# Layer norm on an x that is loaded already turned: TensorE turns the repeated means and deviations instead of x

## The reference

```python
def _layernorm(x, axis=-1, eps=1e-05):
    m = jnp.mean(x, axis=axis, keepdims=True)
    v = jnp.var(x, axis=axis, keepdims=True)
    return (x - m) / jnp.sqrt(v + eps)

# cross attention: 32 query heads, 8 key/value heads, 128 wide, rope on q and k
x = x + jnp.tanh(g_xattn[0]) * xattn(_layernorm(x), ctx, ctx, mask, wq, wk, wv, wo)
# feed-forward: 8 experts of rank 16, the best one alone is used for a token
x = x + jnp.tanh(g_ffn[0]) * ffn(_layernorm(x), route_w, A, Bw)
```

## Time and profile before

| | |
|---|---|
| median of 3 runs | 1053.44 us (1051.94 to 1054.69) |
| the profiled execution's own time | 1052.97 us |
| its span in the profile | 1051.2 us |
| TensorE busy | 1041.9 us, 99% |
| VectorE busy | 872.2 us, 83% |
| ScalarE busy | 634.0 us, 60% |
| GpSimd busy | 592.1 us, 56% |
| TensorE's granted clock | full speed throughout |

### The profile page before, as it was taken

One profiled execution on the slowest core, in us unless ns is written; L12 is line 12 of the kernel. 1 busy time (PEld: TensorE's weight loads), 2 busy tenths in 40 slices (PEclk: granted clock), 3 DMA queues, 4 the chain that ended last, 5 costly groups with the idle time before them and its releaser, 6 DMA issues.

```text
span 1051.2 us, 19131 instructions
## 1 busy us (share of the span) xinstructions
PE 1041.9 (99%) x6663; PEld 865.3 (82%) x6663; DVE 872.2 (83%) x1423; ACT 634.0 (60%) x1112; POOL 592.1 (56%) x518
## 2 busy tenths in 40 slices
PE   9999999999999999999999999999999999999998
PEld 7888888877788888888888888888888888888786
DVE  7875766788888888888888899888887878787997
ACT  6554466676767666767665645556564655555653
POOL 4552379887878787878764533334343434444423
PEclk9999999999999999999999999999999999999999
DMA  7868966565765656565559844654454545443102
GB/s 264 266 223 303 401 221 250 160 261 212 252 214 184 222 180 211 194 199 204 166 221 392 279 144 158 190 182 149 153 175 135 180 145 171 163 147 131 46 26 81
DMA packets 106094, 206.40 MB, mean 196 GB/s; under 512 B 8848, under 2 KB 58640, under 8 KB 100112
## 3 DMA queue, kind: packets, MB, share of 16 engines
q1 hardware_dynamic: 105424, 204.40, 56.8%
q10 hardware_dynamic: 576, 0.79, 0.2%
HBM read 122.31 MB, written 82.84 MB: 195 GB/s over the span
## 4 chain that ended last, share of the span: by engine, by line
PE 89%; DVE 5%; POOL 2%; issue 1%; SPq 1%; DMA 0%; ACT 0%; DVEq 0%; POOLq 0%
PE attn L1003 31%; PE proj L928 26%; PE attn L870 7%; PE turned L870 4%; PE score L870 4%; PE attn L988 3%; PE score L950 3%; PE attn L990 3%; PE turned L963 3%; PE small L950 2%; PE proj L845 1%; DVE acc L1358 1%; POOL rot L1972 1%; PE proj L950 1%; DVE o_s L1346 1%
## 5 line engine op out<-in xcount | busy, mean ns | idle before, releaser
L1003 PE MATMUL attn<-wo_s,o_s 128*128 128x512 f32 x1524 | 375.0, 395 | 0.6 <-DVE o_s L1346 0.5
L928 PE MATMUL proj<-xB,wq_s 128*128 128x512 f32 x1344 | 334.4, 391 | 0.1
L1003 PEld LDWEIGHTS attn<-wo_s,o_s 128*128 128x128 f32 x1524 | 280.8, 188 | 58.5 <-DVE o_s L1346 1.5
L928 PEld LDWEIGHTS proj<-xB,wq_s 128*128 128x128 f32 x1344 | 251.3, 188 | 51.8 <-issue 0.7
L1972 POOL TENSOR_TENSOR rot<-rot,tab 128x512 f32<-128x512 f32 x110 | 162.6, 1478 | 146.6 <-ACT rot L1691 146.4
L1246 DVE TENSOR_TENSOR q_r<-q_r,tab 128x512 f32<-128x512 f32 x127 | 114.2, 899 | 1.5 <-ACT x_third L1691 1.4
L1346 DVE TENSOR_TENSOR o_s<-attn,o_s 128x512 fp32r<-128x512 f32 x127 | 82.5, 685 | 33.9 <-ACT o_s L1740 33.9
L1712 ACT ACTIVATE copies<-proj 128x512 f32<-128x512 f32 x96 | 57.4, 598 | 80.7 <-PE proj L928 80.6
L1740 ACT ACTIVATE o_s<-attn 128x512 fp32r<-128x512 f32 x127 | 69.3, 597 | 57.1 <-PE attn L990 57.1
L1358 DVE SCALAR_TENSOR_TENSOR acc<-attn,gates_t,acc 128x512 f32<-128x512 f32 x127 | 94.9, 748 | 10.2 <-PE attn L1003 7.9
L1972 POOL TENSOR_TENSOR rot_third<-rot_third,tab 128x512 f32<-128x512 f32 x40 | 61.6, 1540 | 57.9 <-ACT rot_third L1691 55.0
(11 more groups left out here) (280 smaller groups left out, 1735.2 us busy)
## 6 DMA issues: line engine op xcount, KB each, us to landing
wq_kept<-wq_s SPq DMA_DIRECT2D x16, 1792.0 KB, 6.6
wq_s<-wq_kept SPq DMA_DIRECT2D x16, 1792.0 KB, 7.7
v_kept<-vst SPq DMA_DIRECT2D x64, 256.0 KB, 4.2
v_s<-v_kept SPq DMA_DIRECT2D x128, 128.0 KB, 5.0
wo_kept<-wo_s SPq DMA_DIRECT2D x32, 512.0 KB, 6.5
wo_s<-wo_kept SPq DMA_DIRECT2D x32, 512.0 KB, 5.5
k_kept<-kst SPq DMA_DIRECT2D x32, 256.0 KB, 2.1
wq_raw<-in_wq SPq DMA_DIRECT2D x16, 512.0 KB, 7.9
```

The lines of the kernel that those rows point to most:

```text
L928: last = e.matmul(dst[:, :], wq_s[:, b % 2, A, s, kt, :], xB[:, B, mv, kt, :], start=(first and kt == 0 and m == 0), stop=(kt == 1 and m = ...
L1003: last = e.matmul(out_bank(k, bp)[:, :], o_s[:, s, bp, h, :], wo_s[n % WO_SLOTS][:, m, :], start=(h == 0 and i == 0), stop=(h == GROUP - 1 ...
```

## The change

x is given to the kernel a second time, as `in_xT`, with features on partitions. This turned form is fetched into the places where x was before. The untouched rows of x are fetched as well, into the memory that the mask and the weights of the experts take later (`x_rows`), and serve only for mean and variance. TensorE no longer turns x. It turns, for each tile, one column with the means and one with the deviations, each repeated 128 times: what comes out has in each of its 128 partitions the row of all tokens' means (or deviations). For the pairs 4 to 7 (`pool_subtracts`) ScalarE copies these rows from PSUM to SBUF, GpSimd subtracts and VectorE multiplies; for the pairs 0 to 3 VectorE does both passes, reading them from PSUM. The mask is fetched at job 34 instead of 12, the experts' weights at 36 instead of 14.

```diff
-X_TURN, X_COMBINE, X_SPLIT = 3, 4, 5
+X_TURN, X_NORM, X_COMBINE, X_SPLIT = 2, 3, 4, 5
-X_FETCH = [6, 8, 9, 14, 28, 29, 31, 33]
+X_FETCH = [7, 8, 10, 14, 28, 29, 31, 33]
+X_STATS = (8, 11, 14, 18, 26, 28, 30, 32)
+ROWS_FETCH = (6, 7, 9, 12, 20, 22, 27, 29)
+MASK_FETCH, ROUTED_FETCH = 34, 36
+def pool_subtracts(pair):
+    return pair >= CHUNK_TILES
...
+        def x_stat(w, which):
+            at = (2 * w[3] + which) * P
+            if pool_subtracts(X_ORDER[x_number(w)]):
+                return stats_s[:, x_number(w) % 2, w[3], which].unsqueeze(1).to_broadcast([P, KT, P])
+            return proj[x_number(w) % 2][:, at:at + P].unsqueeze(1).to_broadcast([P, KT, P])
...
+            def fetch_rows(no):
+                if no >= 2:
+                    e.wait_ge(ln_moments, CHUNKS * (no - 1))
+                for c, w in enumerate(X_PAIRS[X_ORDER[no]]):
+                    e.dma_start(x_rows(no)[:, c, :], x_tiles[x_tile(w)]).then_inc(rows_here(no, c)[0], 16)
...
-            def turn_x(pair):
-                e.wait_ge(ln_done, NORM_NO[X_PAIRS[pair][1]] + 1)
-                for c, w in enumerate(X_PAIRS[pair]):
-                    if X_NO[pair]:
-                        e.wait_ge(x_copied, 2 * X_NO[pair] - 1 + c)
-                    turn(proj[c], 0, x_place(w), cols=KT).then_inc(x_turned, 1)
+            def spread_stats(pair):
+                no = X_NO[pair]
+                e.wait_ge(ln_rstd, CHUNKS * (no + 1))
+                if no >= 2:
+                    e.wait_ge(x_normed, CHUNKS * (no - 1))
+                for c, w in enumerate(X_PAIRS[pair]):
+                    for which in range(2):
+                        at = (2 * c + which) * P
+                        last = e.transpose(proj[no % 2][:, at:at + P],
+                                           x_stats[:, NORM_NO[w], which:which + 1].to_broadcast([P, P]), ident)
+                last.then_inc(stats_spread, 1)
...
+            def x_norms_end(pair):
+                if not pool_subtracts(pair):
+                    e.wait_ge(stats_spread, X_NO[pair] + 1)
+                    for w in X_PAIRS[pair]:
+                        e.wait_ge(*raw_here(w))
+                        e.tensor_tensor(x_by_token(w), x_by_token(w), x_stat(w, 0), ALU.subtract).then_inc(x_less_mean, 1)
+                for w in X_PAIRS[pair]:
+                    e.wait_ge(x_less_mean, NORM_NO[w] + 1)
+                    e.tensor_tensor(x_by_token(w), x_by_token(w), x_stat(w, 1), ALU.mult).then_inc(x_normed, 1)
...
             for n in range(len(JOBS)):
-                if n in X_BESIDE and n < X_LAST:
-                    x_norms_begin(X_BESIDE[n])
+                if n - X_COMBINE in X_BESIDE and pool_subtracts(X_BESIDE[n - X_COMBINE]):
+                    x_norms_end(X_BESIDE[n - X_COMBINE])
+                if n in X_STATS:
+                    x_norms_begin(X_STATS.index(n))
...
+                if n - X_NORM in X_BESIDE and not pool_subtracts(X_BESIDE[n - X_NORM]):
+                    x_norms_end(X_BESIDE[n - X_NORM])
...
-                    e.activation(x_place(w), proj[c][:, :], ACT.Copy).then_inc(x_copied, 1)
+                e.activation(stats_s[:, no % 2].rearrange("p c s t -> p (c s t)"), proj[no % 2][:, :], ACT.Copy).then_inc(
+                    stats_copied, 1)
...
+            def x_less_means(pair):
+                e.wait_ge(stats_copied, X_NO[pair] + 1)
                 for w in X_PAIRS[pair]:
-                    inverse_std(w)
+                    e.wait_ge(*raw_here(w))
+                    e.tensor_tensor(x_by_token(w), x_by_token(w), x_stat(w, 0), ALU.subtract).then_inc(x_less_mean, 1)
...
+                if n - X_NORM in X_BESIDE and pool_subtracts(X_BESIDE[n - X_NORM]):
+                    x_less_means(X_BESIDE[n - X_NORM])
```

More of the change, by code:

```diff
@@ L319, in wo_low_step, with build @@
     return 3 if j == 1 else j
-def build(nc, x, ctx, mask, g_attn, g_ffn, wq, wk, wv, wo, routed_w, lora_b, table, out):
+def build(nc, x, xT, ctx, mask, g_attn, g_ffn, wq, wk, wv, wo, routed_w, lora_b, table, out):
     x_tiles = x.rearrange("b s d -> (b s) d").rearrange("(t p) d -> t p d", p=P)
@@ L1461, in _ @@
                     raw_low(w)
[L1462 removed]
+                if n - X_SPLIT in X_BESIDE:
                     x_lows(X_BESIDE[n - X_SPLIT])
```

149 lines of the change are left out of this document (85 added, 64 removed).

## The result

| | before | after |
|---|---|---|
| median | 1052.8 us (1051.9 to 1054.7, 4 runs) | 1067.6 us (1066.3 to 1068.5, 4 runs) |
| ratio after / before | | 1.0137, 95% interval 1.0118 to 1.0157 |
| span of the profiled execution | 1051.2 us | 1066.3 us |
| TensorE, VectorE, GpSimd busy | 1041.9, 872.2, 592.1 us | 1042.8, 880.0, 600.2 us |
| moved to and from HBM | 206.4 MB | 210.6 MB |

What follows compares the result with a forecast made beforehand. TensorE, busy for 99% of the span, was taken as the bound. Job 42 at +2.55 us, less 0.43 for one later block of turns, gave +2.1 and 1055.1 profiled; forecast 1055.3 us, range 1049.7 to 1058.5.

Steps and rivals of the forecast that it cites:

- TensorE's turns: Eight blocks of turns of x: 4 turns instead of 8 in each, 3.5 us less, alone 1049.5 us.
- The first four pairs: 30 to 85 us: TensorE waits about 2 us after job 20 for the fourth pair's statistics; job 22 at +0.3 us.
- the dear case: Turns after job 20: with GpSimd's subtraction at 1.28 us and VectorE's product waiting it out, TensorE waits 3.1 us.
- From job 22 to 28: Fourth pair's split, expected level with before; job 22 at +0.3 us, between -1.75 and +1.4.
- The last four pairs cost nothing: VectorE's 4 passes a pair replace 2 scalings and the statistics; costed at nothing, covered by TensorE's jobs 45 to 50.
- The full transfers: 86 to 130 us: added rows and mask delay the store awaited with job 38 by 3.95 us; job 42 at +2.55 us.
- Rival 3: Full transfers: SyncE's issuing, not bytes, is the measure; 6.9 us of issuing, +5.1, 1058 us; chance 0.18.
- The wait for the rows of the last pair: Job 32: VectorE takes the last statistics ahead of its values, their rows land late; job 36 at +2.0 us.
- What I gave as proof: Profile signs: TensorE idle after job 20 and ahead of jobs 36, 40, 42; transfer share about 1 from 86 to 135 us.

Runs made afterwards that it cites:

- e12: The kernel before with half of the turns left out in 7 of the 8 pairs (28 turns less); 1052.3 us, ratio 0.9999.
- e1: The kernel after with VectorE subtracting and multiplying for all eight pairs from PSUM, without GpSimd's subtraction and ScalarE's copy; 1062.1 us.
- e3: The kernel after with unused matmuls on TensorE where it would wait, 18 ahead of the turns after job 20 and 10 ahead of job 28; 1067.1 us.
- e5: e1 with the fourth pair's statistics one job earlier in VectorE's list, at job 17; 1061.6 us.
- e9: e5 with the fourth pair's split into high and low parts one job later, at job 24; 1061.0 us.
- e8: e5 with the edits of e6 and e7, and three PSUM banks instead of two for the turned rows; 1058.3 us.
- e10: e8 with the fourth pair's split at job 24 and the last four pairs' statistics at 26, 27, 29, 31, rows at 20, 22, 27, 28; 1057.9 us.
- e11: e10 with the last four pairs' rows fetched at jobs 20, 22, 24, 26 and their statistics at 23, 25, 27, 29; 1057.8 us.
- e14: e10 with the last four pairs' rows at 20, 22, 24, 27, statistics at 23, 26, 28, 30, turned x at 31, 33, 35, 37; 1056.8 us.
- e18: e15 with everything of the fourth pair one job earlier (statistics at job 16, split at 22); 1057.9 us.
- e16: e12 with the fourth pair's split at job 24; 1053.9 us.
- e7: e6 with the last four pairs' rows fetched at jobs 18, 20, 22, 24 and their statistics at 20, 23, 25, 27; 1064.1 us.
- e4: The kernel before with the change's added fetches of rows, used by nobody, and mask and experts' weights fetched at jobs 34 and 36; 1058.3 us.
- e17: e15 with 10 unused matmuls on TensorE ahead of job 28; 1056.7 us.
- e2: The kernel after with the fourth pair's statistics ahead of the third pair's multiplication in VectorE's list at job 18; 1065.9 us.
- e6: The kernel after with mask and experts' weights fetched at jobs 48 and 50 instead of 34 and 36; 1064.5 us.
- e13: The kernel after with the last four pairs' turned x fetched at jobs 31, 33, 35, 37 instead of 28, 29, 31, 33; 1067.0 us.
- e15: e14 with the fourth pair's split at job 23 instead of 24; 1056.2 us.

## Why the prediction was wrong, step by step

- **TensorE's turns**, 3.5 us: held in size (0.36 us for four, the repeated column is as cheap as another). What failed is "alone this would make 1049.5": e12 shows that by itself it is worth next to nothing here (ratio 0.9999 with 28 turns less, 1.3 us at job 51 in the profile), since the first 1.5 us of it end at job 28, which had 0.2 us to spare. I had that number and did not use it for the gain.
- **The first four pairs**, "about 2 us", at most 3.1, and "+0.3 at job 22": the step that failed. Job 22 is at +5.5. The wait was 5.1. Beyond the 3.1 of the dear case it is 0.9 us because the key of job 16 was finished at 62.6 instead of 61.7, and 1.5 because GpSimd's subtraction held up the splits of the second pair (2.1 us without it in e1); TensorE came 0.4 later than I had it (65.7). The fall of the clock, 1.5 us, had no place in the sum; this first one was hidden again by the wait of job 28 (e3).
- **From job 22 to 28** I carried "level with before" forward. A chain of its own runs there: x finished behind the turns, sums, ScalarE's split, the context's split, the key of job 24. It cost 3.0 us and another 1.5 of clock. e5 shows that it does so even when the statistics are in time, and e9 that the place of the split is the cause. Of 15.1 us, 10.1 are lost by job 29, against a forecast of 0.3.
- **"The last four pairs cost nothing"**: failed in a small part. The turns waited 2.4 us for passes that VectorE does in job order; with three banks (e8, e10, e11 and e14 to e18, without e16, which has the old turns) that wait is gone. It is gone in e7 as well, with two banks and earlier statistics, so the banks alone are not shown to be the remedy.
- **The full transfers**, +2.55 at job 42: near for that job (e4: +3.0), and the size of the delay was right (3.95 us forecast for the values of job 38, 4.2 measured). But the path was partly another, since job 39 and the turns wait and not job 42; and the term stopped too early: it left out the experts' weights as lying behind the store of job 34, and they delay the next ones. e4 loses 5.7 us, 1.8 of it at job 46. Rival 3, which forecast 1058 from SyncE's issuing, comes near e4's time by luck: behind the rows, two thirds of its 6.9 us, the stores of the jobs 31 and 32 were issued earlier than before, not later. The wait for the rows of the last pair, foretold at +2.0 for job 36, is real, and larger once TensorE is in time: 3.66 us in e9.
- **What I gave as proof** was mostly there (the wait after job 20, the share of 1.03 from 96 to 144 us, stores late, ScalarE waiting for them). I had named the signs and mis-sized the first by a factor of three with its clock.

What is shown: the causes of both early waits (e1, e5, e9), that the idle time lowers the clock (e3, e17), and that the added transfers alone cost 5.7 us (e4), for the first stores through their landing and not their issue. Open is which transfer exactly sets job 51 when TensorE is early: of e9 to e18, those that reach job 29 earliest are not those that reach job 51 earliest, and I did not find one rule for it.

## What to carry to other kernels

Where an engine is 99% busy but each of its jobs has only 0.2 to 1.4 us to spare against another engine, taking work from it can bring next to nothing by itself; up to the first place with little spare time, that spare time is the measure of the gain. Moving a pass from ahead of a step to behind it is not free though its work is the same: follow everything that stands behind it in each engine's list up to the next place where the busy engine waits. And put the clock into the sum of every wait of some microseconds, but look whether anything later takes it back.

## What the runs showed of the hardware

- TensorE's clock fell after waits of 5.1, 3.7, 3.0, 2.2 and 1.9 us (to 0.50, read in after, e1, e9 and e18), but not after those of 2.1 and 2.0 us at job 28 in e2 and e6: the length of the wait alone does not decide it. Each fall made a job of 12 matmuls 1.1 to 2.6 us longer (4.00 us for job 21 in e13, 5.49 for job 28 in e5, against 2.88), in kernels with the same wait too: after 3.0 us job 28 took 4.44 in after and 5.49 in e13.
- Four turns of a column repeated 128 times start 0.36 us apart from the next block, 0.09 us each.
- Two VectorE passes with one operand in PSUM took 1.27 us beside GpSimd (e5, 75.89) and 1.27 to 1.28 alone (e1, 62.06 and 63.25); two with both in SBUF took 1.28 alone and 2.38 beside GpSimd. GpSimd's pair of subtractions took 2.54 us, and 3.00 beside VectorE's splits.
- From 86 to 130 us the stores of values took a median of 6.3 us from issue to landing before and 9.6 in e4, with 2.1 MB more in flight; in the nearly idle stretch from 60 to 80 us it was 2.8.
- A stretch with the transfer engines full is not slow by itself: e15 has a share of 1.01 from 96 to 144 us and TensorE never waits in it; in after it is 1.03 and TensorE waits.
